# A two-layer triangle-multiplication kernel: the row scales of layer 0's channel normalisation come back from HBM already repeated over the channels

## The reference, cut to what matters

```python
def _ln(x, w, b):                       # layer 0's norms, over the 64 channels of one pixel
    mu, var = mean(x, -1), var(x, -1)
    return (x - mu) * rsqrt(var + 1e-5) * w + b

def layer0(z, ...):                     # z = _gn(x): group norm of the (1, 256, 256, 64) image, 32 groups
    zn = _ln(z, ln_in_w, ln_in_b)
    a = mask * sigmoid(zn @ w_ag + b_ag) * (zn @ w_ap + b_ap)
    b = mask * sigmoid(zn @ w_bg + b_bg) * (zn @ w_bp + b_bp)
    p = einsum('bikc,bjkc->bijc', a, b)
    return (_ln(p, ln_out_w, ln_out_b) @ w_z + b_z) * sigmoid(zn @ w_g + b_g)

x = x + layer0(_gn(x), ...)
x = x + layer1(_gn(x), ...)             # the same in kind, with whole-tensor norms; untouched here
```

## Time and profile before

| | us |
|---|---|
| median of 3 runs (1142.48 to 1143.33) | 1142.88 |
| the profiled execution | 1143.12 |
| its span, first to last instruction | 1140.0 |

### The profile page before, as it was taken

The page is one execution under the profiler, slowest core; times in us unless marked ns, Lnnn a source line. Parts: engine busy times, 40 slices in busy tenths (PEclk is TensorE's granted clock), DMA queues, the critical chain, the costliest instruction groups (busy, mean ns, idle before and its releaser), DMA issues.

```text
span 1140.0 us, 35302 instructions
## 1 busy us (share of the span) xinstructions
PE 1022.2 (90%) x13943; PEld 796.0 (70%) x13948; DVE 787.9 (69%) x1238; ACT 639.1 (56%) x1006; POOL 414.0 (36%) x351
## 2 busy tenths in 40 slices
PE   5569988759999999996999995999999999969997
PEld 4434333329888888985999994788888888735554
DVE  5644988977686868768888888644535454367775
ACT  4556655546565656555676674444535444446665
POOL 0000534668173461904777772000000000046664
PEclk9989999959999999998999997899999999979999
DMA  9930000000211203079998940014041130499995
GB/s 271 288 87 10 0 1 0 1 1 4 112 41 60 92 21 131 4 193 229 228 202 186 211 86 1 3 34 118 4 112 40 53 99 3 131 209 286 283 272 148
DMA packets 209035, 121.29 MB, mean 106 GB/s; under 512 B 70789, under 2 KB 202245, under 8 KB 206857
## 3 DMA queue, kind: packets, MB, share of 16 engines
q1 hardware_dynamic: 208904, 119.34, 41.5%
HBM read 68.99 MB, written 50.33 MB: 105 GB/s over the span
## 4 chain that ended last, share of the span: by engine, by line
PE 78%; DVE 9%; SPq 3%; issue 3%; DMA 3%; POOL 2%; ACT 2%; DVEq 0%; POOLq 0%; another core or an unknown queue 0%; ACTq 0%
PE PS L466 70%; SPq L334 3%; PE PS L726 2%; PE PS L711 2%; PE PS L758 2%; DMA AB<-x 2%; DVE AB L1205 1%; POOL XT_ALL L953 1%; POOL AB L320 1%; DVE XT_ALL L1226 1%; DMA AB<-k_scratch 1%; DVE XT_ALL L1387 1%; DVE WK L1262 0%; DVE REC L1379 0%; PE PS L480 0%
## 5 line engine op out<-in xcount | busy, mean ns | idle before, releaser
L466 PE MATMUL PS<-EFF,XT_ALL 64*128 64x64 f16 (+1 forms) x10368 | 343.6, 201 | 7.0 <-POOL XT_ALL L953 3.6
L466 PE MATMUL PS<-AB 128*128 128x256 f32 (+2 forms) x1221 | 319.4, 411 | 30.6 <-ACT AB L814 10.6
L466 PEld LDWEIGHTS PS<-EFF,XT_ALL 64*128 64x128 f16 (+1 forms) x10368 | 316.5, 97 | 41.0 <-issue 15.2
L466 PEld LDWEIGHTS PS<-AB 128*128 128x128 f32 (+2 forms) x1226 | 223.6, 185 | 123.5 <-ACT AB L814 28.8
L842 ACT ACTIVATE WK<-PS,T 128x512 f32<-128x512 f32 x256 | 175.5, 687 | 143.4 <-PE PS L466 131.5
L1014 POOL TENSOR_TENSOR WK<-XT_ALL 128x512 f32 (+1 forms) x64 | 83.9, 1313 | 351.2 <-DMA k_scratch<-WK 304.5
L320 POOL TENSOR_TENSOR AB<-WK,MS 128x512 f32 x96 | 130.6, 1388 | 105.6 <-DVE WK L1262 105.5
L953 POOL TENSOR_TENSOR XT_ALL<-AB,XT_ALL 128x512 f32 (+1 forms) x59 | 69.8, 1191 | 179.3 <-DVE XT_ALL L1226 169.0
L1267 DVE TENSOR_TENSOR AB<-PS,WK 128x512 f32 x128 | 87.6, 691 | 65.0 <-ACT WK L842 64.3
L1262 DVE TENSOR_TENSOR WK<-PS,WK 128x512 f32<-128x512 f32 x128 | 86.8, 689 | 31.2 <-ACT WK L842 24.5
L1284 DVE BATCH_NORM_STATS2 REC<-WK 128x512 f32 x64 | 44.4, 694 | 82.1 <-ACT WK L866 82.1
(11 more groups left out here) (190 smaller groups left out, 1407.3 us busy)
## 6 DMA issues: line engine op xcount, KB each, us to landing
AB<-x SPq DMA_DIRECT2D x64, 512.0 KB, 7.1
p_scratch<-WK SPq DMA_DIRECT2D x32, 512.0 KB, 2.6
k_scratch<-WK SPq DMA_DIRECT2D x128, 128.0 KB, 1.9
AB<-k_scratch SPq DMA_DIRECT2D x32, 512.0 KB, 7.7
out<-AB SPq DMA_DIRECT2D x16, 1024.0 KB, 6.1
AB<-p_scratch SPq DMA_DIRECT2D x29, 512.0 KB, 7.5
AB<-p_scratch SPq DMA_DIRECT2D x2, 640.0 KB, 6.3
RAW<-w SPq DMA_DIRECT2D x2, 256.0 KB, 2.6
```

The source lines that it names most:

```text
L466: return nc.tensor.matmul(dst, lhsT, rhs, start=start, stop=stop)
```

## The change

**The sums.** A quad is four groups. The squares have four buffers, and `variances` issues for each quad four matmuls of 32 columns, one per group, each into its own 32 partitions of the bank (output rows 32j to 32j + 31 for group j of the quad). The three copies are gone. PE's order is now four centrings, then the quad's four sums (at the second quad with the folding of the weights between them). The rounds are five, of 16, 16, 16, 8 and 8 groups, and use banks 4 and 5 in turn.

**The row operations.** Epsilon, root, reciprocal and the three refining operations stay, now on 128 partitions (L1208, L1211 to L1214 of the new kernel). The split into bf16 parts, the constant `spread` with its load, and the spreading matmuls are gone. DVE issues the row operations of round t before the last four groups of round t - 1 (so: groups 0 to 11, rows, groups 12 to 27, rows, 28 to 43, rows, 44 to 51, rows, 52 to 63).

**The way back.** SP stores the rows to HBM with four DMAs (`store_rows`), waits for them, and loads each quad with two DMAs (`load_scales`): 63 partitions by four groups by 512 values, from a source that repeats over the partitions. Partition 0 of each half is set to 256 by POOL beforehand. There are four quad buffers: two in `WK`, two in `AB`, the latter over part of what was `zn`, which now has four buffers.

**The groups.** DVE multiplies `XT_ALL` by the quad's buffer in SBUF. The high part is no longer a copy but `tensor_tensor(max)` of `zn` with itself. DVE may write `zn` again when the low part of four groups before is done. In the last 12 groups (`TAIL`) ACT makes the high parts, and DVE takes the low parts of groups 52, 55, 58 and 61.

The loops of this stage are written out instead of being `Fori` loops, except POOL's.

```diff
-SPREAD_LAG = 5
-TG = 16
-NT = NG // TG
+QD = 4
+SIZES = (16, 16, 16, 8, 8)
+STARTS = tuple(sum(SIZES[:t]) for t in range(len(SIZES)))
+NT = len(SIZES)
+TAIL = 12
...
-        zn = xs.rearrange("p s r m -> p (s r m)")[:, 0:8 * BANK].rearrange("p (s n) -> p s n", s=8)
+        zn = flat[:, 0:4 * BANK].rearrange("p (s n) -> p s n", s=4)
+        sq = flat[:, 4 * BANK:8 * BANK].rearrange("p (s n) -> p s n", s=4)
...
+            def store_rows(t):
+                sp.wait_ge(rows_ready, t + 1)
+                k0, k1 = STARTS[t] // QD, (STARTS[t] + SIZES[t]) // QD
+                for j in range(QD):
+                    sp.dma_start(r_dram[j, 2 * k0:2 * k1, :], rt[32 * j:32 * j + 2 * (k1 - k0), :]
+                                 ).then_inc(rows_stored, 16)
+
+            def load_scales(t):
+                sp.wait_ge(rows_stored, 16 * QD * (t + 1))
+                for k in range(STARTS[t] // QD, (STARTS[t] + SIZES[t]) // QD):
+                    if k < 4:
+                        sp.wait_ge(rb_set, 4)
+                    else:
+                        sp.wait_ge(zn_done, QD * (k - 3))
+                    for q in range(2):
+                        rows = r_dram[:, 2 * k + q, :].unsqueeze(0).to_broadcast([CH - 1, QD, BANK])
+                        dst = scale_quad(k)[q * CH + 1:(q + 1) * CH, :].rearrange("p (j n) -> p j n", j=QD)
+                        sp.dma_start(dst, rows).then_inc(rb_in[k % 4], 16)
...
-                mm(PS[:, 5 + u % 2, :], spread_sb[:, u * P:(u + 1) * P], parts3).then_inc(bc_done, 1)
...
-                        mm(PS[0:96, 4, :], NCF[:, s0:s0 + 96], sq[:, v % 2], v == 0, v == TG - 1).then_inc(mm2_done, 1)
...
+                for j in range(QD):
+                    n = STARTS[t] + QD * a + j
+                    pe.wait_ge(sq_ready, n + 1)
+                    nc.tensor.matmul(PS[32 * j:32 * j + 32, 4 + t % 2, :], NCF[:, s0:s0 + 32], sq[:, n % 4],
+                                     start=a == 0, stop=a == SIZES[t] // QD - 1).then_inc(mm2_done, 1)
...
+            for k, (t, a) in enumerate(quads):
+                for j in range(QD):
+                    centre(QD * k + j)
+                if k == 1:
+                    fold_weights()
...
+                variances(t, a)
...
+            def normalise(n):
+
+                k = n // QD
+                if n % QD == 0:
+                    dve.wait_ge(rb_in[k % 4], 32 * (k // 4 + 1))
+                if n >= 4:
+                    dve.wait_ge(*low_done(n - 4))
+                dve.wait_ge(zc_done, n + 1)
+                V.tensor_tensor(zn[:, n % 4], XT[:, n * GR:(n + 1) * GR, :].rearrange("p r n -> p (r n)"),
+                                scale_quad(k)[:, n % QD * BANK:(n % QD + 1) * BANK], ALU.mult).then_inc(zn_done, 1)
+                if 0 < n <= NG - TAIL:
+                    high(n - 1)
...
-                V.tensor_copy(half(n, 0), zn[:, slot]).then_inc(hi_done, 1)
+                V.tensor_tensor(half(n, 0), zn[:, n % 4], zn[:, n % 4], ALU.max).then_inc(hi_done, 1)
...
+            for t in range(1, NT):
+                for n in range(max(STARTS[t - 1] - QD, 0), STARTS[t] - QD):
+                    normalise(n)
+                row_scales(t)
+            for n in range(STARTS[NT - 1] - QD, NG):
+                normalise(n)
```

More of the change, by code:

```diff
@@ L83, with build @@
 V_LNW, V_LNB, V_OW, V_OB, V_AI, V_BI, V_AO, V_BO, V_N = range(9)
-def build(nc, x, mask, w0, w1, bias0, bias1, vecs, consts, norm_consts, spread, ones3, out):
+def build(nc, x, mask, w0, w1, bias0, bias1, vecs, consts, norm_consts, ones3, out):
     f32 = mybir.dt.float32
@@ L297, in new_x_bank, with low_done @@
             return g % 2 + (0 if isinstance(g, int) and g >= NG - 2 else 2)
-        LOWS_V = [u for u in range(TG) if u % 3 == 1]
-        def low_count(u):
-            return NG - TG + sum(v not in LOWS_V for v in range(u + 1))
+        LOWS_V = [n for n in range(NG - TAIL, NG) if n % 3 == 1]
+        def low_done(n):
+            if n in LOWS_V:
+                return lo_done_v, LOWS_V.index(n) + 1
+            return lo_done, n + 1 - sum(m <= n for m in LOWS_V)
         MASKS_V = (1,)
@@ L567, in _ @@
+            quads = [(t, a) for t in range(NT) for a in range(SIZES[t] // QD)]
+            for k, (t, a) in enumerate(quads):
[3 more added lines that the diff above has]
+                    fold_weights()
+                if k == 2:
+                    small([(PS[:, 7, P:2 * P], ones, diag),
+                           (PS[:, 7, 2 * P:2 * P + 1], out_sq, ones[:, 0:1])])
+                variances(t, a)
             for layer in range(2):
@@ L949, in _, with low @@
         def _(pool):
[L951 to L960 removed]
+            def low(n, slot):
+                nc.gpsimd.tensor_tensor(half(n, 1), zn[:, slot], half(n, 0), ALU.subtract).then_inc(lo_done, 1)
+            for tile in (rb_wk, rb_ab):
+                for q in range(2):
+                    if tile is rb_ab and q == 0:
+                        pool.wait_ge(tr_done, NG)
+                    nc.gpsimd.memset(tile[q * CH:q * CH + 1, :, :], Z_SCALE).then_inc(rb_set, 1)
+            with pool.Fori(0, (NG - TAIL) // 4) as t:
+                for u in range(4):
+                    pool.wait_ge(hi_done, t * 4 + (u + 1))
+                    low(t * 4 + u, u)
+            for n in range(NG - TAIL, NG):
+                if n not in LOWS_V:
+                    pool.wait_ge(hi_done_a, n + 1 - (NG - TAIL))
+                    low(n, n % 4)
             with pool.Fori(0, NQ) as q:
@@ L1460, in shape_constants @@
     norm[:, L_DROP:L_DROP + P] = (eye - (same & (c[:, None] == 0))) * (c[None, :] != 0)
-    for part in range(3):
-        norm[k, L_SEL + 30 + 32 * part + par] = 1 / CH
+    norm[k, L_SEL + 30 + par] = 1 / CH
     norm[k, L_ECOL + CH * par] = 1
```

191 lines of the change are left out of this document (63 added, 128 removed).

## The result

| | us |
|---|---|
| before, median of 4 runs (1142.22 to 1143.33) | 1142.68 |
| after, median of 4 runs (1191.19 to 1193.43) | 1193.07 |
| ratio, with its 95% interval | 1.0437 (1.0424 to 1.0449) |
| forecast, and its range | 1195 (1155 to 1216) |
| span of the profiled execution after | 1189.2 |

What follows compares the result with a forecast made beforehand. The normalisation stage's end was taken to bound the kernel, with DVE and POOL excluding each other. Row operations, HBM trips and groups over five rounds move it from 249.6 to 301.5: 1142.9 + 51.9 = 1195 us, range 1155 to 1216.

Steps and rivals of the forecast that it cites:

- What bounds: Normalisation stage: the change is worth what it moves the end of POOL's last low half, at 249.58 us.
- The slow start of PE: PE just behind the stage: already there before the change, at granted clock 0.56, so counted at nothing.
- The group, 2.17: DVE and POOL per group: three mutually exclusive operations, 0.55 + 0.60 + 1.02 = 2.17 us; 12 groups take 25.0.
- The row operations: DVE, start of each round: without the split 6.9 us in five rounds, where it was 11.0 in four.
- R, 12.7: Way over HBM, from last row operation to first usable quad: 12.7 us; a quad behind it follows 5.5 later.
- PE and ACT: Squares and sums before row operations: 7.8 us a quad, row operations begin at 109.3, later squares cost nothing.
- The sum: Stage end: rounds 0 to 2 at 44.6 us each, round 3 at 27.3, then the last, ending at 301.5.
- the tail: End of round 4: four multiplications and a low half on DVE, three low halves on POOL, 6.0 us.
- The signs: Expected in the changed trace: POOL's subtraction 1.5 to 1.7 us, L1234 over 1, row operations 6.9, projections near 301.
- Rival 1, nine engines: Scale loads of 63 partitions use nine DMA engines, a load takes 4.3 us: 1209 us in all, chance 0.28.
- Rival 2, sharing: DVE and POOL work side by side after all, a group takes 1.25 us: 1161 us in all, chance 0.12.
- Rivals 3 and 4: Port shared: HBM way at 7.2 us gives 1143, chance 0.04; shorter still is faster, 1136 at 5, chance 0.08.

Runs made afterwards that it cites:

- e12_both: Changed kernel with cast for maximum, multiplication's second input from constant PSUM banks, and scale loads taken from x without waiting for stores: 1132.76 us.
- e2_lows_dve: Changed kernel with the low halves of groups 0 to 51 moved from POOL to DVE: 1182.22 us.
- e9_copy_48_15: Changed kernel with a cast in place of the maximum and each 63-partition load split into 48 and 15 partitions: 1174.73 us.
- e1_copy: Changed kernel with the high half made by a cast again instead of the maximum: 1183.05 us.

## Why the prediction was right, step by step

- *What bounds:* right. The change is worth what it moves the end of the stage: 49.8 us, where the spans of the same two executions differ by 49.2. The slow start of PE, put at nothing, was a little faster (clock 0.73 for 0.56).
- *The group, 2.17:* right to 0.01, both in the period and in its parts: 0.56, 0.60 and 1.02 were measured for 0.55 (the mask tiles, another stage), 0.60 and 1.02 (this stage). The Trainium skill's rule (SBUF — State Buffer, SBUF: two separate sides), whole durations in turn, would have made it 2.5 by the prediction's estimate. The trace has the exclusion, but 0.08 to 0.14 us of each operation lies outside. A run of 12 groups, priced at 25.0, took 23.5, 25.0 and 25.0 (the first run has only 11 maxima in it), and the four groups of round 3 took 7.7, as priced.
- *The row operations:* right, 6.9 from L1208's start to L1214's end. That they had cost four times 11.0 was true of the first round alone (11.0, 13.0, 12.5, 10.8); the sum does not use it.
- *R, 12.7:* 12.6, 12.4, 13.5, 12.9 and 13.1. The mean, 12.9, is near, but by two errors that nearly cancel, which is luck. In the first round the stores took 2.5, not 3.5 (16 KB each, not 128 KB as in the earlier trace rows), and the loads 10.1, not 9.2. The last quad came after 6.25, not 5.5. That nothing is queued on SP behind the new DMAs was wrong: the load of the weights is, at 277.71; what it cost is not known.
- *PE and ACT:* too slow on my paper. A quad took 7.3 (ACT's L832 starts at 92.13 and 99.42), since ACT's two operations overlap by a tenth, and the folding cost ACT 3.75 with its start under other work; row operations began at 105.7, not 109.3. Later squares never held DVE up, as said, and without the two costs they did once (3.1 in `e12_both`).
- *The sum:* forecast end 301.5, measured 299.4. Too late by 3.6 at the start and by 1.5 in the runs of groups; too early by 0.9 in the five R, by 0.8 in the last quad, and by 1.3 in the tail (7.3 for 6.0: in the chain above, a multiplication of 1.65 behind POOL and ACT's high half of 0.64 stand between, where I had counted only DVE and POOL). So the mechanism and the two large terms were right, and that the total is off by only 2 owes something to luck: 5.1 us of error one way, 3.0 the other.
- *The signs:* L1234 at 1.64, row operations of 6.9 and the projections from 299.5 came as said. POOL's subtraction took 1.40, not 1.5 to 1.7: it starts 0.30 behind DVE's multiplication, and only 0.19 in the earlier trace rows. The waits of rounds 1 to 3 were 4.7, 5.8 and 5.2, not 4, partly because the four groups in hand lasted 7.8, not 8.7: the first of them meets no POOL.
- *Rival 1, nine engines:* its mechanism is there, 0.56 of sixteen engines, as the rule of the Trainium skill on how a DMA is split (DMA: Bandwidth & Descriptors, Why a DMA increments its semaphore by 16 and not by 1) has it. Its price was wrong: I had let the time of a load grow as 16/9, to 4.3, and a further load took 2.8 to 3.1, because with nine a packet takes less time (0.10 for 0.15 us). As a forecast of R, 15.0, it was 2.1 off, mine 0.2.
- *Rival 2, sharing:* false. POOL ran at 1.40 and L1234 at 1.64, and `e2_lows_dve` is faster with POOL idle.
- *Rivals 3 and 4* needed sharing and an R of 7.2 or less; neither came near.
- *The part I did not price by itself:* what is left without exclusion and trip gains 10.0 us. That the terms 5 x 6.9 for 4 x 11.0 make 9.5 is near it by chance, since the start, the waits for spreads and the last groups changed as well.

A part of the harm need not come with the idea: 10.0 us for a maximum in place of a cast, 8.6 for loads of 63 partitions, 18.3 together (`e9_copy_48_15`). The other 32 us of the 50.4 stayed: the second SBUF input and the rest of the trip, less the 10.0 gained.

## What to carry to other kernels

Look in the timeline of the kernel that you have for the same pair of operations on DVE and POOL, in another stage too: the end-to-end distances there (0.55, 0.60, 1.02) gave the period here to a hundredth. Where they exclude each other, let one read PSUM, or give the work to one engine. The trip of these rows over HBM took 12.4 to 13.5 us until its first use, once per dependent round; work put under it covers only as long as that work lasts, so making the work faster gives back less than it saves. Try the parts of a large change by themselves: what was left of this one was worth 10.0 us, and a kernel that keeps most of it, with the rows on the chip, beat both.

## What was not expected of the hardware

- With 0.56 to 0.60 of the sixteen DMA engines' time in use the loads moved 155 and then 189 GB/s, with all of it 179 to 200. Using all of them gave a quarter more at the start of a round and little behind it.
- A cast, with one SBUF input, waits for POOL's two-input operation too, but ends 0.29 behind it (`e1_copy`: POOL ends at 136.03, the cast at 136.32), where a maximum ends 0.56 behind.
- Sums in four column tiles do start together when all squares are there, eight instructions in 1.07 us:

```profile
89.97 1.07 PE L578 MATMUL PS<-AB 128*32 128x512 f32 x8
```

In the later quads the last sum waits for the last squares. What the tiles give by themselves was not tried.
